# Layer 1 of a four-layer kernel in another order: the first sigmoid ahead of the last latent copy, the recurrence output turned into other banks, gelu two tiles ahead of the rounding

## The chip, the cores and the metric

The kernel runs on one core of a Trainium2 chip. The metric is the device time of one execution in microseconds (us). Each engine (TensorE, here PE; VectorE, DVE; ScalarE, ACT; GpSimd, POOL; and the DMA issuer SP) runs its own instructions in order and waits on semaphores for the others.

## What is computed

Four layers work on `x`, 1024 tokens (4 batches of 256) of 256 channels. Each begins with a recurrence over the tokens (the same `k = v = fside` in all layers, another decay and bonus in each), whose result does not depend on `x`:

```python
base = sigmoid(x) * num / max(den, 1e-8)     # num, den: forward and backward scans plus a bonus term
cond = base * (0.8 + 0.2 * tf)               # tf = sigmoid(sum(time_emb)), one number per batch
x = x + ffn_l(cond)
```

The ffn of layer 0 routes 32 small experts and adds shared ones, that of layer 2 routes 8 experts, that of layer 3 is a ternary gated one. The ffn of layer 1, which the change is about, is

```python
q, s1 = quantize_rowwise(cond)               # round(cond * 127 / absmax of the row)
h = gelu((q @ W1q.T) * (s1 * sW1 / 127**2) + b1)     # 256 -> 1024
q2, s2 = quantize_rowwise(h)                 # the row's absmax over 1024 numbers
y = (q2 @ W2q.T) * (s2 * sW2 / 127**2) + b2          # 1024 -> 256
```

## The kernel before, in words

Everything is written out by hand: the order of each engine's instructions is the order of the code in its block (`sync`, `gpsimd`, `scalar`, `vector`, `tensor`), and semaphores with counts tie the engines together. There are eight PSUM banks of 128x512 f32.

Layer 0 ends in 64 expert units. Unit u uses `bank[u % 4]` for its up-projection; `expert_y` (L1597) adds all units into banks 4 (first half of the tokens) and 5 (second half). `latent_copy(s)` (ACT, L689) copies bank 4+s, `latent_out(s)` (PE, L1612) multiplies it into two banks of two token tiles each, and `add_routed(v)` (DVE, L1121) adds bank v to `x` and counts `x1_ready`, to 4.

Then layer 1 starts. `sigmoid_x(1, (s,))` (ACT, L605) takes the sigmoid of half s of `x`. `turn_gain(1, b)` (PE, L1477) turns batch b's recurrence output back to tokens x channels, in `gain_bank(1, b)`, and `make_cond(1, b)` (DVE, L939) multiplies the two to `cond` (it counts `cond_ready`). `row_scales(s)` (DVE, L1164 to L1167) finds the row maxima of a half, four tiles.

A tile t of 128 tokens (NT = 8 of them) goes through:
- POOL `quant_rows` (L462) rounds it to `qf`; PE `turn_rows` (L1663) turns it into bank 4; ACT `l1_first` (L715) copies it to `qT`; PE `first` (L1676) multiplies it into banks 0, 1 (even t) or 2, 3 (odd t).
- DVE `l1_pre` (L1174, two halves) scales it and adds the bias; ACT `l1_gelu` (L721) writes `gl`.
- DVE `l1_scales` (L1183 to L1186) finds the row maximum; ACT `l1_quant` (L726) rounds `gl` in place; PE `turn_hidden` (L1687) turns it into banks 5 and 6; ACT `l1_second` (L734, two halves) copies it to `q2T`; PE `second` (L1696) multiplies it into bank 7; DVE `l1_out` (L1191) adds it to `x` and counts `x2_ready`.

POOL adds the bias b2 to `x` meanwhile (L473). `xp`, `qf`, `qT`, `q2T` and `gl` have two buffers each. ACT must load a table (ACT_TABLE_LOAD) when it goes from one of exp, sigmoid and gelu to another; copies need none. DVE also finishes here the last block of the recurrence of layers 1 and 2 (`gain_reciprocal` L923 and `gain_out` L929). Behind the last tiles come sigmoid and cond of layer 2 (`sigmoid_pair` L622, `make_cond(2, b)`), whose gains are turned into banks 0 to 3, and its routing, whose first vector instruction is the copy of the logits (L1236). Those go on in one chain to the 23 expert blocks of layer 2.

Of the kernel before, what the change touches and what calls it, by code (L numbers as in the profile page):

```python
# [58 lines left out]
def build(nc, x_d, kt_d, te_d, w_d, u_d, sm_d, gbias_d, down_d, fc2_d, w1_d, w2_d,  # L59
          q1_d, q1b_d, q2_d, q2b_d, rt_d, gu_d, dn_d, t1_d, t2_d, t3_d, cond_d, y_d, cw_d, out_d):  # L60
    with ExitStack() as ctx:
# [802 lines left out]
        def _(dve):  # L864
# [334 lines left out]
            for t in range(-3, NT + 1):  # L1199
                if 0 <= t + 1 < NT and t != 0:  # L1200
                    l1_pre(t + 1)
                if t == -2:
                    add_routed(2)
                    add_routed(3)
                if t == -1:
                    make_cond(1, 2)
                    make_cond(1, 3)
                if 0 <= t < NT:
                    l1_scales(t)
                if t == 0:  # L1210
                    l1_pre(1)
                    row_scales(1)
# [691 lines left out]
```

## Time and profile before

| | |
|---|---|
| time, median of 3 runs | 499.85 us (499.19 to 500.91) |
| the profiled execution | 499.61 us, of it 497.9 us in the profile's span |
| PE busy | 396.2 us, 80% of the span |
| DVE busy | 353.4 us, 71% |
| ACT busy | 229.9 us, 46% |
| POOL busy | 229.9 us, 46% |
| granted TensorE clock, mean of the span | 0.938 of full speed |

Busy time says how long an engine ran instructions, and no engine is busy all the time, so the shares alone do not say what sets the end: in each stage it is a chain that goes from engine to engine. The layer-0 experts run to about 207 us of the span, layer 1 from there to about 260 us, the routing of layer 2 to about 288 us, its expert blocks to about 440 us, and layer 3 to the end.

### The profile page before, as it was taken

The page shows a single profiled execution, that of the slowest core. Times are in us where ns is not written, and L with a number is a line of the kernel's source. Part 1 is how long each engine was busy: PE and PEld are TensorE (multiplying, and loading weights), DVE is VectorE, ACT ScalarE, POOL GpSimd, SP SyncE. Part 2 cuts the span into 40 slices and gives each one's busy share as a digit, 9 for nine tenths or more (in the row PEclk, how much of TensorE's full clock was granted, in tenths as well). Part 3 has the DMA queues.
Part 4 walks back from the last instruction along what each step waited for, and adds up shares of the span by engine and source line. Part 5 has one row for each costly group of instructions (what it writes and reads, how often), then busy time and mean ns, then how long its engine had stood idle before and what let it go on. Part 6 is the DMA issues. An engine that isn't in the chain of part 4 may idle for free.

```text
span 497.9 us, 5689 instructions
## 1 busy us (share of the span) xinstructions
PE 396.2 (80%) x1636; PEld 252.3 (51%) x1636; DVE 353.4 (71%) x643; ACT 229.9 (46%) x448; POOL 229.9 (46%) x313
## 2 busy tenths in 40 slices
PE   0866877999989999856765289999999999914795
PEld 0645655855555555534454135655555555612453
DVE  5999679899999999469854727655655421148995
ACT  4400174266766766537783113333333333235884
POOL 3116140468778996222200145785785551104642
PEclk9998899999999999979995569999999999975999
DMA  7900000536656643000011389889889887150001
GB/s 229 366 1 0 1 0 2 201 127 199 197 195 198 224 149 128 0 1 1 1 44 42 130 301 349 296 297 379 292 284 396 294 279 304 40 180 1 11 33 43
DMA packets 23262, 77.37 MB, mean 155 GB/s; under 512 B 3424, under 2 KB 7904, under 8 KB 19648
## 3 DMA queue, kind: packets, MB, share of 16 engines
q1 hardware_dynamic: 19936, 69.94, 39.4%
q0 software_dynamic: 2208, 6.03, 4.0%
q10 hardware_dynamic: 1088, 1.05, 0.6%
q8 instruction: 13, 0.21, 0.2%
q14 instruction: 17, 0.14, 0.1%
HBM read 71.76 MB, written 5.24 MB: 155 GB/s over the span
## 4 chain that ended last, share of the span: by engine, by line
PE 47%; DVE 33%; issue 7%; ACT 6%; DMA 4%; POOL 1%; SPq 0%; DVEq 0%; ACTq 0%; POOLq 0%
PE bank L1792 17%; PE bank L1812 9%; PE bank L1603 6%; DVE fw L915 4%; DVE hx L1130 4%; DVE bw L918 3%; DVE fw L923 2%; DVE fw L977 2%; PE bank L1803 2%; DVE gl L1418 2%; PE bank L1460 2%; PE bank L1462 2%; PE bank L1461 2%; DVE pt L1425 1%; DVE cond L939 1%
## 5 line engine op out<-in xcount | busy, mean ns | idle before, releaser
L1792 PE MATMUL bank<-gu,xbT 128*128 128x512 f32 x184 | 85.8, 610 | 0.9 <-ACT xbT L774 0.9
L1603 PE MATMUL bank<-hx,w2raw 128*128 128x512 f32 x128 | 67.1, 607 | 4.2 <-DVE hx L1130 3.8
L1333 DVE TENSOR_TENSOR hm<-bank,sl 128x512 f32<-128x512 f32 x23 | 15.9, 691 | 70.7 <-PE bank L1792 39.5
L680 ACT ACTIVATE rl<-bank 128x512 f32<-128x512 f32 x64 | 38.1, 595 | 39.5 <-PE bank L1462 38.8
L1792 PEld LDWEIGHTS bank<-gu,xbT 128*128 128x128 f32 x184 | 35.6, 196 | 37.2 <-issue 34.7
L1460 PE MATMUL bank<-xlhi,w1hi 128*128 128x512 f32 x64 | 49.5, 773 | 1.1 <-DVE hx L958 1.1
L1812 PE MATMUL bank<-dn,hT 128*128 128x256 f32 x184 | 45.2, 388 | 3.5 <-ACT hT L785 0.8
L1130 DVE TENSOR_TENSOR hx<-bank,cwb 128x512 f32<-128x512 f32 x64 | 41.9, 657 | 6.5 <-ACT bank L684 4.8
L490 POOL DMA_INDIRECT y_rows<-yb,dest_i x23 | 25.0, 1088 | 41.6 <-ACT yb L791 41.0
L923 DVE RECIPROCAL fw<-fw 128x256 f32<-128x256 f32 x24 | 41.5, 1730 | 0.0
L415 POOL TENSOR_TENSOR fw<-fw,bw 128x256 f32<-128x256 f32 x32 | 24.1, 752 | 34.7 <-DVE bw L918 34.3
L483 POOL DMA_INDIRECT xb<-cond_rows,row_i x23 | 26.4, 1148 | 28.7 <-PE bank L1778 15.1
L1812 PEld LDWEIGHTS bank<-dn,hT 128*128 128x128 f32 x184 | 33.1, 189 | 11.8 <-issue 8.2
L684 ACT ACTIVATE bank<-rl 128x512 f32<-128x512 f32 x64 | 38.1, 596 | 0.0
L1541 PE MATMUL bank<-fw,ident 128*128 128x256 f32 x32 | 12.9, 493 | 25.4 <-DVE bw L918 12.4
L1603 PEld LDWEIGHTS bank<-hx,w2raw 128*128 128x128 f32 x128 | 22.3, 188 | 16.0 <-DVE hx L1130 10.0
L779 ACT ACTIVATE sl<-bank 128x512 f32<-128x512 f32 x23 | 13.7, 597 | 34.6 <-PE bank L1792 34.6
L785 ACT ACTIVATE hT<-bank 128x256 f32<-128x256 f32 x46 | 15.1, 381 | 29.4 <-PE bank L1803 29.4
L791 ACT ACTIVATE yb<-bank 128x256 f32<-128x256 f32 x23 | 8.8, 384 | 37.2 <-PE bank L1812 37.2
L419 POOL TENSOR_TENSOR fw<-fw,eu 128x256 f32<-128x256 f32 x32 | 23.9, 748 | 3.5
L1687 PE MATMUL bank<-ident,gl 128*128 128x128 f32 x128 | 17.2, 277 | 10.4 <-ACT gl L726 8.3
L1461 PE MATMUL bank<-xllo,w1hi 128*128 128x512 f32 x64 | 25.3, 395 | 0.0
(283 smaller groups left out, 907.7 us busy)
## 6 DMA issues: line engine op xcount, KB each, us to landing
gu<-in_gu SPq DMA_DIRECT2D x23, 1024.0 KB, 7.3
cwb<-cw_rows SPq DMA_DIRECT2D x32, 512.0 KB, 3.8
dn<-in_dn SPq DMA_DIRECT2D x23, 512.0 KB, 4.5
traw<-in_t SPq DMA_DIRECT2D x3, 1024.0 KB, 7.9
w1raw<-in_w SPq DMA_DIRECT2D x8, 256.0 KB, 4.8
w2raw<-in_w SPq DMA_DIRECT2D x8, 256.0 KB, 5.0
kT<-in_kt SPq DMA_DIRECT2D x4, 256.0 KB, 5.5
x<-in_x SPq DMA_DIRECT2D x2, 512.0 KB, 6.9
```

Source lines behind the costliest of these rows:

```text
L415: pool.tensor_tensor(fw[:, p, d, :], fw[:, p, d, :], bw[:, p, d, :], ALU.add).then_inc(sem("both_" + part), 1)
L483: pool.indirect_dma_start(xb[:, b % RING, :], None, cond_d, bass.IndirectOffsetOnAxis(ap=row_i[:, b:b + 1], axis=0)).then_inc(sem(f"xb_in{ ...
L490: pool.indirect_dma_start(y_d, bass.IndirectOffsetOnAxis(ap=dest_i[:, b:b + 1], axis=0), yb[:, b % 2, :], None).then_inc(sem(f"y_out{b % 2 ...
L680: act.activation(rl[:, u % 3, :], bank[u % 4][:], ACT.Relu).then_inc(sem("r_ready"), 1)
L684: act.activation(bank[u % 4][:], rl[:, u % 3, :], ACT.Square).then_inc(sem("sq_ready"), 1)
L923: dve.reciprocal(fw[:, p, 1, :], fw[:, p, 1, :]).then_inc(sem("rden_ready"), 1)
L1130: dve.tensor_tensor(hx[:, 0, u % 4, :], bank[u % 4][:], cwb[:, e % CRING, HALF * s:HALF * s + HALF], ALU.mult).then_inc(sem("h0_ready"), 1)
L1460: pe.matmul(out, lhs[0], rhs[0], start=start, stop=False)
L1461: pe.matmul(out, lhs[0], rhs[1], start=False, stop=False)
L1603: pe.matmul(bank[4 + s][:], w2raw[:, e // 4 % 2, e % 4, :], hx[:, 0, u % 4, :], start=(e == 0), stop=(e == E0 - 1), skip_group_check=True) ...
L1792: ins = pe.matmul(bank[2 * (b % 2) + up][:], xbT[:, b % 2, k, :], gu[:, b % RING, k, up * I2:up * I2 + I2], start=(k == 0), stop=(k == KC ...
L1812: ins = pe.matmul(y_bank(b), hT2[:, b % 2, j, :], dn[:, b % RING, j, :], start=(j == 0), stop=(j == 3))
```

## The change

ACT. The sigmoid table is loaded right behind the last expert's square, and the first half's sigmoid is taken before the second latent copy instead of after it. In the tile loop gelu of tile t+2 comes right behind the rounding of tile t, ahead of the copies of tile t (before: gelu of t+2 behind the copies of t, right ahead of the rounding of t+1). `gl` now has three buffers in layer 1 and `pt` a third column. The table for layer 2's sigmoid is loaded inside the loop, at t = 5, and the sigmoids of its first two batches are taken before the rounding of the last tile.

PE. The gains of layer 1 go to banks 0, 1, 6, 2 (before 2, 3, 5, 6); all four are turned before `latent_out(1)`, two of them between the last `expert_y`. Rows are turned and multiplied one tile further ahead, four tiles instead of three. DVE. `add_routed(2)` and `(3)`, the last reciprocal and `gain_out` stand before the first `l1_pre`, `row_scales(1)` before the first `l1_scales`, and in the loop `l1_scales` and `l1_pre` run one tile further ahead of `l1_out`. POOL waits for the last `expert_y` before it rounds rows.

```diff
-            return bank[((0, 1, 1, 7), (2, 3, 5, 6), (0, 1, 2, 3), (0, 1, 5, 6))[l][b]]
+            return bank[((0, 1, 1, 7), (0, 1, 6, 2), (0, 1, 2, 3), (0, 1, 5, 6))[l][b]]
...
+            pool.wait_ge(sem("y_done"), UNITS)
...
+            load_table(5, ACT.Sigmoid)
+            sigmoid_x(1, (0,))
             latent_copy(1)
-            sigmoid_x(1, (0,))
...
-                wait(act, sem("q2t_ready"), 2 * t - 2)
+                wait(act, sem("q2t_ready"), 2 * t - 4)
                 act.wait_ge(sem("pre_ready"), t + 1)
...
-            for t in range(-2, NT):
+            l1_first(0)
+            sigmoid_x(1, (1,))
+            load_table(1, ACT.Gelu_apprx_tanh)
+            l1_first(1)
+            l1_gelu(0)
+            l1_first(2)
+            l1_gelu(1)
+            l1_first(3)
+            for t in range(NT):
+                l1_quant(t)
                 if t + 2 < NT:
-                    l1_first(t + 2)
-                if t == -2:
-                    sigmoid_x(1, (1,))
-                    load_table(1, ACT.Gelu_apprx_tanh)
-                if t == 0:
-                    l1_quant(t)
-                if 0 <= t + 1 < NT:
-                    l1_gelu(t + 1)
-                if t > 0:
-                    l1_quant(t)
-                if t == NT - 1:
+                    l1_gelu(t + 2)
+                if t + 3 == NT:
+                    load_table(6, ACT.Sigmoid)
+                l1_second(t)
+                if t + 4 < NT:
+                    l1_first(t + 4)
+                if t == NT - 2:
                     sigmoid_pair(2, 0)
                     sigmoid_pair(2, 1)
-                if t >= 0:
-                    l1_second(t)
...
-                wait(dve, sem("q2_ready"), t - 1)
+                wait(dve, sem("q2_ready"), t - 2)
+                wait(dve, sem("x2_ready"), t - 2)
                 dve.wait_ge(sem("gelu_ready"), t + 1)
...
+            add_routed(2)
+            add_routed(3)
+            gain_reciprocal(3 * NBLK - 1, 1)
+            gain_out(3 * NBLK - 1, 2, NBLK - 1, 1)
+            l1_pre(0)
+            make_cond(1, 2)
+            make_cond(1, 3)
+            l1_pre(1)
+            row_scales(1)
+            l1_scales(0)
+            l1_pre(2)
+            for t in range(NT):
+                if t + 1 < NT:
+                    l1_scales(t + 1)
+                if t + 3 < NT:
+                    l1_pre(t + 3)
                 if t >= 1:
                     l1_out(t - 1)
...
-                if u == UNITS - 2:
-                    turn_gain(1, 0)
-            turn_gain(1, 1)
+                if u >= UNITS - 3 and u < UNITS - 1:
+                    turn_gain(1, u - UNITS + 3)
+            turn_gain(1, 2)
+            turn_gain(1, 3)
             latent_out(1)
-            pe.wait_ge(sem("x1_ready"), 3)
-            turn_gain(1, 2)
-            pe.wait_ge(sem("x1_ready"), 3)
-            turn_gain(1, 3)
...
+            pe.wait_ge(sem("x1_ready"), 1)
             turn_rows(0, "", "q1_ready")
+            l1_up(0)
+            turn_rows(1, "", "q1_ready")
+            pe.wait_ge(sem("cond_ready"), 8)
+            l1_up(1)
+            turn_rows(2, "", "q1_ready")
+            l1_up(2)
+            turn_rows(3, "", "q1_ready")
+            l1_up(3)
+            pe.wait_ge(sem("x1_ready"), 4)
+            for t in range(NT):
+                turn_hidden(t, "", "q2_ready")
+                if t + 4 < NT:
+                    turn_rows(t + 4, "", "q1_ready")
                 if t == NT - 2:
                     pe.wait_ge(sem("pre_ready"), NT)
-                    turn_gain(2, 0)
...
+                second(t, "", "x2_ready", lambda c: q2w[:, c, :])
+                if t + 4 < NT:
+                    l1_up(t + 4)
```

What stands in a row on ACT where layer 1 starts, before, from the square of the last expert unit on (`ylat` is the latent copy, `cond<-x` the sigmoid of a half, `qT` the copy of turned rows, `gl<-xp` gelu, `gl<-gl,pt` the rounding):

```order
L684 ACTIVATE bank3<-rl_100 128x512 [waits r_ready]
L689 ACTIVATE ylat_107<-bank5 128x512 [waits y_done]
L605 ACT_TABLE_LOAD
L605 ACTIVATE cond_57<-x_50 128x1024 [waits x1_ready]
L715 ACTIVATE qT_121<-bank4 128x256 [waits q1t_ready]
L605 ACTIVATE cond_57<-x_50 128x1024 [waits x1_ready]
L588 ACT_TABLE_LOAD
L588 ACTIVATE table_65<-wl_67 128x1
L715 ACTIVATE qT_121<-bank4 128x256 [waits q1t_ready]
L721 ACTIVATE gl_123<-xp_122 128x1024 [waits pre_ready]
L715 ACTIVATE qT_121<-bank4 128x256 [waits m1_ready,q1t_ready]
L726 ACTIVATE gl_123<-gl_123,pt_77 128x1024 [waits q2_scale]
```

And in the changed kernel, from the same square on (every line number is up to 5 higher here):

```order
L685 ACTIVATE bank3<-rl_100 128x512 [waits r_ready]
L589 ACT_TABLE_LOAD
L589 ACTIVATE table_65<-wl_67 128x1
L606 ACTIVATE cond_57<-x_50 128x1024 [waits x1_ready]
L690 ACTIVATE ylat_107<-bank5 128x512 [waits y_done]
L717 ACTIVATE qT_121<-bank4 128x256 [waits q1t_ready]
L606 ACTIVATE cond_57<-x_50 128x1024 [waits x1_ready]
L589 ACT_TABLE_LOAD
L589 ACTIVATE table_65<-wl_67 128x1
L717 ACTIVATE qT_121<-bank4 128x256 [waits q1t_ready]
L723 ACTIVATE gl_123<-xp_122 128x1024 [waits pre_ready]
L717 ACTIVATE qT_121<-bank4 128x256 [waits m1_ready,q1t_ready]
```

The table load and the first sigmoid have moved ahead of the second latent copy, and the sigmoid no longer stands behind a wait for the last `expert_y`. The next place is ACT in the tile loop, from one rounding to the next, before:

```order
L726 ACTIVATE gl_123<-gl_123,pt_77 128x1024 [waits q2_scale]
L734 ACTIVATE q2T_124<-bank5 128x512 [waits q2t_ready,m2_ready]
L734 ACTIVATE q2T_124<-bank6 128x512 [waits q2t_ready]
L715 ACTIVATE qT_121<-bank4 128x256 [waits m1_ready,q1t_ready]
L721 ACTIVATE gl_123<-xp_122 128x1024 [waits pre_ready,q2t_ready]
L726 ACTIVATE gl_123<-gl_123,pt_77 128x1024 [waits q2_scale]
```

And in the changed kernel:

```order
L728 ACTIVATE gl_123<-gl_123,pt_77 128x1024 [waits q2_scale]
L723 ACTIVATE gl_123<-xp_122 128x1024 [waits pre_ready,q2t_ready]
L736 ACTIVATE q2T_124<-bank5 128x512 [waits q2t_ready,m2_ready]
L736 ACTIVATE q2T_124<-bank6 128x512 [waits q2t_ready]
L717 ACTIVATE qT_121<-bank4 128x256 [waits m1_ready,q1t_ready]
L728 ACTIVATE gl_123<-gl_123,pt_77 128x1024 [waits q2_scale]
```

Gelu has moved from ahead of the rounding to behind it: it now lies between the rounding of a tile and the copies of that tile, for which PE has to turn the tile. The third place is DVE where layer 1 starts, before, from the adds of the second half (`x<-bank5`) to the first row maximum of gelu's output and the pre-activation behind it:

```order
L1121 TENSOR_TENSOR x_50<-bank5,x_50 128x512 [waits fo_ready,dve_step]
L1121 TENSOR_TENSOR x_50<-bank7,x_50 128x512 [waits fo_ready]
L1174 SCALAR_TENSOR_TENSOR xp_122<-bank0,st_76,b1bc_63 128x512 [waits m1_ready]
L1174 SCALAR_TENSOR_TENSOR xp_122<-bank1,st_76,b1bc_63 128x512
L939 SCALAR_TENSOR_TENSOR cond_57<-bank5,tfb_71,cond_57 128x512 [waits sig_ready,G_turned]
L939 SCALAR_TENSOR_TENSOR cond_57<-bank6,tfb_71,cond_57 128x512 [waits sig_ready,G_turned]
L1183 TENSOR_REDUCE pt_77<-gl_123 128x1 [waits gelu_ready]
L1184 RECIPROCAL pt_77<-pt_77 128x1 [waits dve_step]
L1185 TENSOR_SCALAR pt_77<-pt_77,ws_78 128x1 [waits dve_step]
L1186 TENSOR_SCALAR pt_77<-pt_77 128x1
L1174 SCALAR_TENSOR_TENSOR xp_122<-bank2,st_76,b1bc_63 128x512 [waits m1_ready]
L1174 SCALAR_TENSOR_TENSOR xp_122<-bank3,st_76,b1bc_63 128x512
```

And in the changed kernel:

```order
L1126 TENSOR_TENSOR x_50<-bank5,x_50 128x512 [waits fo_ready,dve_step]
L1126 TENSOR_TENSOR x_50<-bank7,x_50 128x512 [waits fo_ready]
L928 RECIPROCAL fw_55<-fw_55 128x256 [waits sum_den]
L934 SCALAR_TENSOR_TENSOR GT_53<-fw_55 128x256 [waits rden_ready,sum_num]
L1179 SCALAR_TENSOR_TENSOR xp_122<-bank0,st_76,b1bc_63 128x512 [waits m1_ready]
L1179 SCALAR_TENSOR_TENSOR xp_122<-bank1,st_76,b1bc_63 128x512
L944 SCALAR_TENSOR_TENSOR cond_57<-bank6,tfb_71,cond_57 128x512 [waits sig_ready,G_turned]
L944 SCALAR_TENSOR_TENSOR cond_57<-bank2,tfb_71,cond_57 128x512 [waits sig_ready,G_turned]
L1179 SCALAR_TENSOR_TENSOR xp_122<-bank2,st_76,b1bc_63 128x512 [waits m1_ready]
L1179 SCALAR_TENSOR_TENSOR xp_122<-bank3,st_76,b1bc_63 128x512
L1169 TENSOR_REDUCE st_76<-cond_57 128x4 [waits cond_ready]
L1170 RECIPROCAL st_76<-st_76 128x4 [waits dve_step]
```

Behind these rows come two small ones of `row_scales(1)` and then the first `l1_scales`. So the reciprocal, its output step, the pre-activation of tile 1 and the row scales of the second half have all moved ahead of it.

## Rows read from the trace of the kernel before

**Rows 1.** Busy times in windows of the span; after PE's come the clock and DMA.
```profile
212.00:214.00 2.00, 0.00 (x0) 0.00 (x0) 1.90 (x5) 0.00 (x0) 0.29 (x1) 0.61 0.00 0
...
218.00:219.00 1.00, 1.00 (x4) 0.38 (x2) 0.00 (x0) 0.98 (x2) 0.00 (x0) 0.50 0.00 0
...
240.00:250.00 10.00, 7.72 (x56) 5.28 (x56) 8.37 (x16) 7.77 (x13) 0.00 (x0) 1.00 0.00 0
```

**Rows 2.** Timeline of the start of layer 1: start us, us, instruction, idle and releaser.
```profile
202.32 1.11 ACT L684 ACTIVATE bank<-rl 128x512 f32<-128x512 f32 x2
...
204.15 1.28 DVE L1121 TENSOR_TENSOR x<-bank,x 128x512 f32<-128x512 f32 x2
...
206.37 1.02 PE L1603 MATMUL bank<-hx,w2raw 128*128 128x512 f32 x2
...
207.43 0.60 ACT L689 ACTIVATE ylat<-bank 128x512 f32<-128x512 f32 x1 [3.99 <-PE bank L1603]
...
208.04 1.28 ACT L605 ACT_TABLE_LOAD   x1
...
208.08 1.99 PE L1612 MATMUL bank<-fc2w,ylat 128*128 128x256 f32 x8 [0.25 <-ACT ylat L689]
...
209.34 1.06 ACT L605 ACTIVATE cond<-x 128x1024 f32<-128x1024 f32 x1
...
210.53 1.41 DVE L939 SCALAR_TENSOR_TENSOR cond<-bank,tfb,cond 128x512 f32<-128x512 f32 x2 [5.11 <-ACT cond L605]
...
211.98 1.22 DVE L1164 TENSOR_REDUCE st<-cond 128x4 f32<-128x1024 f32 x1
...
213.78 1.29 DVE L1121 TENSOR_TENSOR x<-bank,x 128x512 f32<-128x512 f32 x2
```

**Rows 3.** Timeline of the first two tiles of layer 1.
```profile
217.40 1.89 PE L1676 MATMUL bank<-q1w,qT 128*128 128x512 bf16 x4 [0.48 <-ACT qT L715]
...
219.32 1.41 DVE L1174 SCALAR_TENSOR_TENSOR xp<-bank,st,b1bc 128x512 f32<-128x512 f32 x2 [4.25 <-PE bank L1676]
...
220.13 1.04 PE L1676 MATMUL bank<-q1w,qT 128*128 128x512 bf16 x4 [0.57 <-ACT qT L715]
...
221.97 1.21 DVE L1183 TENSOR_REDUCE pt<-gl 128x1 f32<-128x1024 f32 x1
...
223.72 1.15 ACT L726 ACTIVATE gl<-gl,pt 128x1024 f32<-128x1024 f32 x1 [1.62 <-DVE pt L1186]
...
229.78 1.15 ACT L726 ACTIVATE gl<-gl,pt 128x1024 f32<-128x1024 f32 x1 [0.52 <-DVE pt L1186]
```

**Rows 4.** Timeline of the last reciprocal of the recurrence, on DVE.
```profile
233.01 1.74 DVE L923 RECIPROCAL fw<-fw 128x256 f32<-128x256 f32 x1
...
235.20 0.48 DVE L1191 SCALAR_TENSOR_TENSOR x<-bank,pt,x 128x256 f32<-128x256 f32 x1
```

**Rows 5.** Timeline of a tile in the middle of the loop, from rounding to rounding.
```profile
242.80 1.16 ACT L726 ACTIVATE gl<-gl,pt 128x1024 f32<-128x1024 f32 x1
...
244.76 1.09 ACT L734 ACTIVATE q2T<-bank 128x512 bf16<-128x512 f32 x2 [0.80 <-PE bank L1687]
...
245.50 1.03 PE L1696 MATMUL bank<-q2w,q2T 128*128 128x256 bf16 x8 [0.18 <-ACT q2T L734]
...
245.73 0.39 ACT L715 ACTIVATE qT<-bank 128x256 bf16<-128x256 f32 x1
...
246.00 1.07 ACT L721 ACTIVATE gl<-xp 128x1024 f32<-128x1024 f32 x1
...
246.94 1.16 ACT L726 ACTIVATE gl<-gl,pt 128x1024 f32<-128x1024 f32 x1
```

**Rows 6.** Timeline of the end of layer 1 and the first copy of layer 2's logits.
```profile
255.10 1.28 ACT L622 ACT_TABLE_LOAD   x1
...
259.25 0.48 DVE L1191 SCALAR_TENSOR_TENSOR x<-bank,pt,x 128x256 f32<-128x256 f32 x1 [0.71 <-PE bank L1696]
...
269.61 0.22 DVE L1236 COPY lgs<-bank 128x64 f32<-128x64 f32 x1 [6.27 <-PE bank L1735]
```

More of the change, by code:

```diff
@@ L107, in build @@
         b2bc = sb("b2bc", [P, C])
-        table = sb("table", [P, 5])
+        table = sb("table", [P, 7])
         te = sb("te", [P, B, 64])
@@ L718, in l1_gelu @@
                 p = t % 2
-                wait(act, sem("q2t_ready"), 2 * t - 2)
+                wait(act, sem("q2t_ready"), 2 * t - 4)
                 act.wait_ge(sem("pre_ready"), t + 1)
-                act.activation(gl[:, p, :], xp[:, p, :], ACT.Gelu_apprx_tanh).then_inc(sem("gelu_ready"), 1)
+                act.activation(gl[:, t % 3, :], xp[:, p, :], ACT.Gelu_apprx_tanh).then_inc(sem("gelu_ready"), 1)
             def l1_quant(t):
-                p = t % 2
+                p = t % 3
                 act.wait_ge(sem("q2_scale"), t + 1)
@@ L1190, in l1_out @@
                 dve.wait_ge(sem("xb_ready"), t + 1)
-                dve.scalar_tensor_tensor(out=x[:, t, :], in0=bank[7][:, 0:C], scalar=pt[:, 3, t % 2:t % 2 + 1],
+                dve.scalar_tensor_tensor(out=x[:, t, :], in0=bank[7][:, 0:C], scalar=pt[:, 3, t % 3:t % 3 + 1],
                                          in1=x[:, t, :], op0=ALU.mult, op1=ALU.add).then_inc(sem("x2_ready"), 1)
@@ L1198, in _ @@
             row_scales(0)
[L1199 to L1212, printed above, removed]
-                if t == 2:
-                    gain_reciprocal(3 * NBLK - 1, 1)
-                    gain_out(3 * NBLK - 1, 2, NBLK - 1, 1)
+            add_routed(2)
[14 more added lines that the diff above has]
+                    l1_pre(t + 3)
                 if t >= 1:
                     l1_out(t - 1)
-                if t == NT - 1:
-                    make_cond(2, 0)
-                    make_cond(2, 1)
+            make_cond(2, 0)
+            make_cond(2, 1)
+            l1_out(NT - 1)
             make_cond(2, 2)
@@ L1472, in turn_gain @@
                     pe.wait_ge(sem("y_ready"), NB)
-                elif b >= 2 and l < 2:
-                    pe.wait_ge(sem("cond_ready"), 4 * l + b - 1)
+                elif l == 0 and b == 3:
+                    pe.wait_ge(sem("cond_ready"), 2)
+                elif l == 1 and b == 2:
+                    pe.wait_ge(sem("x1_ready"), 2)
                 for u in range(2):
@@ L1686, in turn_hidden @@
                         c = 4 * h + j
-                        ins = pe.transpose(bank[5 + h][:, j * P:j * P + P],
-                                           gl[:, t % (3 if tag else 2), c * P:c * P + P], ident[:])
+                        ins = pe.transpose(bank[5 + h][:, j * P:j * P + P], gl[:, t % 3, c * P:c * P + P], ident[:])
                     ins.then_inc(sem("q2t_ready" + tag), 1)
@@ L1699, in _, with l1_up @@
             w_first = [lambda k, h=h: q1w[:, k, 512 * h:512 * h + 512] for h in range(2)]
+            def l1_up(t):
+                first(t, "", w_first, lambda p: (2 * p, 2 * p + 1))
+            pe.wait_ge(sem("x1_ready"), 1)
             turn_rows(0, "", "q1_ready")
[L1701 to L1706 removed]
+            l1_up(0)
[11 more added lines that the diff above has]
+                    turn_rows(t + 4, "", "q1_ready")
                 if t == NT - 2:
                     pe.wait_ge(sem("pre_ready"), NT)
[L1710 to L1719 removed]
+                    for b in range(B):
+                        turn_gain(2, b)
+                second(t, "", "x2_ready", lambda c: q2w[:, c, :])
+                if t + 4 < NT:
+                    l1_up(t + 4)
             def turn_cond2(b):
```

19 lines of the change are left out of this document (2 added, 17 removed).

## Prediction
> **What bounds the kernel now.** I read the windows of the span first, then the timeline of layer 1 from the last expert to the logits of layer 2, following from each instruction that had waited to what released it. The window in the tile loop shows PE busy 7.72, DVE 8.37 and ACT 7.77 us of 10 at full clock [rows 1]: no engine is full, so a chain between engines sets the pace. Three pieces of it are what the change touches.
>
> The start [rows 2]: the last `expert_y` ends at 207.39, the latent copy follows, then a sigmoid table and the first sigmoid, to 210.40. DVE has waited 5.11 us for it. Yet the half of `x` that this sigmoid reads was complete at 205.43 (204.15 + 1.28), and ACT had been free since 203.43. So this stretch is order, not work. From there conds, row scales and the first tile lead to the first rounding at 223.72 [rows 3], my first mark.
>
> The first tiles [rows 3]: from the rounding of tile 0 to that of tile 1 there are 6.06 us, since between the two `l1_scales` DVE does two pre-activations and the second half's row scales.
>
> The loop [rows 5]: a tile takes 4.14 us, 242.80 to 246.94, and on ACT it is closed: rounding 1.16, then idle 0.80 while PE turns the tile, copies 0.97 (244.76 to 245.73), the row copy 0.27, gelu 0.94. At the end a table load (255.10) lies between the last tile's rounding and its copies; the last `l1_out` starts at 259.25, and the first logits copy follows 10.36 later [rows 6].
>
> **The change part by part.** I take marks and lay the changed order out with the durations of the rows. Instructions of one engine that don't wait overlap by some 0.1 us, as gelu's 0.94 between starts shows; a handover costs 0.04, on PE's multiplications 0.14.
>
> *Start to the first rounding.* ACT: table 1.28 and the small activation 0.2 from 203.43, free at 204.93, so the sigmoid starts when `x` is there, 205.47, ends 206.55. PE turns two gains between the experts (0.43 each, so the last `expert_y` ends at 207.83 instead of 207.39; that is the price of moving them, and it delays only the second half). DVE: conds 206.59 to 208.0, row scales 1.80 (211.98 to 213.78 before) to 209.8. Rows reach PE at 210.3, where `latent_out(1)`, 207.83 + copy 0.64 + 1.99, is just done at 210.5. This is 4 us earlier than before. Then DVE becomes late: adds to 211.2, reciprocal and its output 2.19 [rows 4], so `l1_pre(0)` only at 213.4 although its product is there at 212.5; 1.33 for it, 1.40 for conds 2 and 3, to 216.1. Now the new banks cost something: the product of tile 1 writes bank 2, which holds the gain of batch 3, and has to wait for that cond: 216.1 + 0.14 + 1.04 = 217.3 (a PE that has stood idle since about 212.7). Then `l1_pre(1)` 1.33, row scales 1.80, `l1_scales(0)` 1.71 (221.97 to 223.68 before) give 222.2 for the first rounding. **Gain 1.5 us**, of the 4 that the sigmoid won; the rest is work brought ahead, paid back next.
>
> *Rounding 0 to rounding 1.* Ahead of `l1_scales(1)` now lies only `l1_pre(2)`. Scales end at 225.1, and ACT has rounding 0, gelu 2 (from 223.5, after `l1_pre(2)`), copies and row copy to do first: 223.5 + 0.95 + 0.97 + 0.27 = 225.7. That is 3.5 us instead of 6.06: **gain 2.5**.
>
> *Rounding 1 to rounding 5*, before 229.78 to 246.94, 17.16 us, the reciprocal of rows 4 in it. With gelu in ACT's gap, ACT alone would need 1.03 + 0.95 + 0.97 + 0.27 = 3.2, and DVE 1.33 + 1.63 + 0.40 = 3.4 per tile. But another loop closes. `second(t)` writes bank 7 and waits for `l1_out(t-1)`, and in the new order `l1_out` stands behind `l1_pre(t+3)`, whose product comes on PE behind `second(t-1)`. Its length: `second` 1.03 less 0.15 of overlap, product 1.04, `l1_pre` 1.33, `l1_out` 0.48, handovers 0.16: **3.9 us a tile**. Laid out, the roundings come at 225.7, 229.0 (ACT's own 3.3), 233.7 (4.7, for `l1_out(0)` stands behind two scales and two pre-activations and ends at 229.8), 237.6, 241.2: 15.5 us. **Gain 1.7**.
>
> *Rounding 5 to the last `l1_out`*, before 12.31. The third table load, 1.28 + 0.1, moves from behind the last rounding to ahead of the copies of tile 5, with nothing to cover it there; the two sigmoids (1.06) lie ahead of the last rounding instead of behind it. Rounding 6 at 245.6, rounding 7 at 249.6, last `l1_out` at 253.4: 12.2. **Gain 0.1**: the stretch loses in front what it wins behind. Conds 0 and 1 of layer 2 are then made ahead of the last `l1_out`, as before. The rest, 10.36 to the logits copy, keeps its order, and I cost it at nothing. POOL's new wait costs nothing, since its rounding waits for row scales later than that anyway; the third `gl` buffer costs no time.
>
> Sum 1.5 + 2.5 + 1.7 + 0.1 = 5.8, with the roundings 5.9.
>
> **The clock.** Before, PE did nothing in 212 to 214, granted clock 0.61, and the first tile's product ran at 0.50 in 1.89 us; the next took 1.04 [rows 1, 3]. In the changed kernel PE stands idle 3.6 us from 212.7. If the clock then drops to the lower level (1.2 of 2.4 GHz), the product of tile 1 costs 0.85 more on the path: gain 5.0. If it does not, 5.9. The Trainium skill ("TensorE: Matmul & The Clock Gate", Part 1) says that the throttled clock is the default and activity releases it, which speaks for a drop here; row and rule agree that an idle PE comes first. I take the middle, 5.4.
>
> **Table loads, weighed.** The row of the load shows 1.28 between copy end 208.03 and sigmoid start 209.34: nothing further [rows 2]. The Trainium skill ("ScalarE: Activation LUTs", "What ACT_TABLE_LOAD costs") adds a drain of about 1.38 us to its 1.28 for every switch. By the row the sum stays; by the page about 1.4 would be added at the load inside the loop and 0.7 at the start, a gain near 3.4.
>
> The profiled execution took 499.61, 0.24 under the median of 499.85. 499.61 - 5.4 = 494.2; against the median 494.45. I say 494.3.
>
> **The rivals.**
> A, as laid out: 493.5 to 495.2. Chance 0.62.
> B, the loop does not get shorter: some wait that I can't see keeps 4.14 a tile, the lag of `l1_out` for instance. Then the gain is 1.5 + (6.06 - 4.14) + (17.16 - 4 x 4.14) + 0.1 = 4.1 at full clock, 3.2 with the drop: 495.6 to 496.4. For it: banks 0 to 3 and 7 are still single. Against: the gap of 0.80 on ACT is filled. Chance 0.14.
> C, a load stalls ACT by more than its row, say its 1.28 once more in the loop and 0.7 at the start, since it now follows gelu with no pause and a copy waits right behind: gain 3.4, 496.1. Against: the row of the load before, with 0.01 on either side. The page named above is the one that would have it so. Chance 0.04.
> D, the loop runs at DVE's own 3.4 a tile because handovers on the bank-7 loop are shorter: 2 us more gain, or later stages fall better to the clock: 492.3 to 493.5. Chance 0.12.
> E, slower: the clock falls in the loop. The bank-7 loop holds 1.9 us of PE work, which doubles: 3.9 becomes 5.8 a tile. Three tiles at that level eat the gain (3 x 1.9 = 5.7), the five from tile 2 on would give 499.6 - 5.4 + 9.5 = 503.7. Against: in the loop before the clock is 1.00 with PE busy 77% [rows 1], and its share rises with 3.9 instead of 4.14. Chance 0.03.
> F, no change: the expert blocks of layer 2 start late for another reason, or fall worse to the clock by as much. Chance 0.05; speaks against it that from `l1_out` to the logits copy is one chain [rows 6].
>
> **How the numbers follow.** Time of A, 494.3. The range leaves out E, F and the far end of D, and takes in the two ends of the clock, B and C: 492.7 to 496.5. What a measurement here can tell from no change is about 0.3%, 1.5 us; A to D all lie beyond. Faster 0.92, same 0.05, slower 0.03.
>
> **What would show it.** First sigmoid at about 205.5; conds at 206.6; DVE without its 5.11 wait; PE idle some 3.5 us before the product of tile 1, released by cond; first rounding at 222.2 to 223.1; no wait of ACT for the turned tile or little; `second` waiting for `l1_out`; roundings 3.9 apart in the middle; a table load ahead of the copies of tile 5; last `l1_out` at 253.4 to 254.3. It is wrong if the roundings stay 4.1 apart, if `l1_pre(0)` doesn't find DVE late, or if the clock is at 0.50 beyond the first tile.

## The result and the profile after

The changed kernel takes 495.31 us in the median of 11 runs (492.86 to 497.70), the kernel before 500.36 in the runs beside it (498.89 to 502.61). The ratio is 0.9905, with a 95% interval of 0.9881 to 0.9929: 0.95% or 4.75 us faster, more than the 0.3% that can be told from no change. The forecast was 494.3 (492.7 to 496.5). The profiled execution took 494.82 us, its span 493.1, where that of before had 499.61. Two timed runs that lie over 1.5% above the fastest of their kernel, at a lower mean clock, are left out of every ratio and median below: one of the kernel before (507.44 us) and one of e2 (566.60 us).

The first section of its page (busy time, share of the span, instructions):

```profile
PE 397.6 (81%) x1630; PEld 255.4 (52%) x1636; DVE 355.6 (72%) x643; ACT 230.4 (47%) x450; POOL 230.8 (47%) x313
```

Busy times are as before to within some 2 us: work was moved, not removed. Its timeline at the start of layer 1:

```profile
203.21 1.11 ACT L685 ACTIVATE bank<-rl 128x512 f32<-128x512 f32 x2
204.34 1.28 ACT L589 ACT_TABLE_LOAD   x1
205.04 1.28 DVE L1126 TENSOR_TENSOR x<-bank,x 128x512 f32<-128x512 f32 x2
205.63 0.20 ACT L589 ACTIVATE table<-wl 128x1 f32<-128x1 f32 x1
206.35 1.06 ACT L606 ACTIVATE cond<-x 128x1024 f32<-128x1024 f32 x1 [0.52 <-DVE x L1126]
207.55 1.41 DVE L944 SCALAR_TENSOR_TENSOR cond<-bank,tfb,cond 128x512 f32<-128x512 f32 x2 [1.23 <-ACT cond L606]
208.75 0.60 ACT L690 ACTIVATE ylat<-bank 128x512 f32<-128x512 f32 x1 [1.34 <-PE bank L1610]
...
212.04 1.74 DVE L928 RECIPROCAL fw<-fw 128x256 f32<-128x256 f32 x1
...
217.21 1.33 PE L1678 MATMUL bank<-q1w,qT 128*128 128x512 bf16 x4 [3.64 <-DVE cond L944]
...
219.44 1.89 PE L1678 MATMUL bank<-q1w,qT 128*128 128x512 bf16 x4 [0.48 <-ACT qT L717]
...
223.46 1.15 ACT L728 ACTIVATE gl<-gl,pt 128x1024 f32<-128x1024 f32 x1 [1.47 <-DVE pt L1192]
```

The sigmoid now waits for `x` and for nothing else; DVE's wait for it has shrunk from 5.11 us [rows 2] to 1.23. The reciprocal of [rows 4] stands at 212.04, ahead of the first tile, and PE is idle for 3.64 us until a cond frees the bank of tile 1's product. A tile in the middle of the loop, in the same timeline:

```profile
234.95 1.16 ACT L728 ACTIVATE gl<-gl,pt 128x1024 f32<-128x1024 f32 x1
235.08 1.05 PE L1697 MATMUL bank<-q2w,q2T 128*128 128x256 bf16 x8 [0.81 <-DVE x L1197]
235.97 1.03 PE L1678 MATMUL bank<-q1w,qT 128*128 128x512 bf16 x4
235.99 1.06 ACT L723 ACTIVATE gl<-xp 128x1024 f32<-128x1024 f32 x1
237.03 1.41 DVE L1179 SCALAR_TENSOR_TENSOR xp<-bank,st,b1bc 128x512 f32<-128x512 f32 x2 [0.19 <-PE bank L1678]
237.53 1.08 ACT L736 ACTIVATE q2T<-bank 128x512 bf16<-128x512 f32 x2 [0.47 <-PE bank L1689]
238.35 0.48 DVE L1197 SCALAR_TENSOR_TENSOR x<-bank,pt,x 128x256 f32<-128x256 f32 x1
238.76 1.16 ACT L728 ACTIVATE gl<-gl,pt 128x1024 f32<-128x1024 f32 x1
238.89 1.05 PE L1697 MATMUL bank<-q2w,q2T 128*128 128x256 bf16 x8 [0.80 <-DVE x L1197]
```

3.81 us from rounding to rounding (234.95, 238.76), where [rows 5] had 4.14. `second` (L1697) waits 0.8 us for `l1_out` (L1197), and a ring, a chain of waits that ends where it began, closes in those rows: 0.89 to the product, 1.06 to `l1_pre`, 1.32 to `l1_out`, 0.54 to the next `second`. And the end of the loop:

```profile
244.42 1.28 ACT L589 ACT_TABLE_LOAD   x1
245.82 1.06 ACT L736 ACTIVATE q2T<-bank 128x512 bf16<-128x512 f32 x2
246.55 1.03 PE L1697 MATMUL bank<-q2w,q2T 128*128 128x256 bf16 x8 [1.93 <-ACT q2T L736]
...
248.91 1.91 PE L1484 MATMUL bank<-ident,GT 128*128 128x128 f32 x16
...
254.51 0.48 DVE L1197 SCALAR_TENSOR_TENSOR x<-bank,pt,x 128x256 f32<-128x256 f32 x1 [0.98 <-PE bank L1697]
...
264.88 0.23 DVE L1241 COPY lgs<-bank 128x64 f32<-128x64 f32 x1 [6.27 <-PE bank L1741]
```

The windows of the same stretches (columns as in [rows 1]) show the clock at 0.72 and 0.58 around the first tiles and at 1.00 in the loop:

```profile
216.00:222.00 6.00, 3.88 (x12) 1.63 (x12) 4.47 (x9) 2.75 (x4) 0.37 (x1) 0.72 0.00 1
224.00:228.00 4.00, 3.25 (x16) 2.91 (x17) 3.93 (x9) 3.54 (x6) 0.71 (x2) 0.58 0.01 2
240.00:250.00 10.00, 6.65 (x54) 5.38 (x53) 6.57 (x17) 8.69 (x13) 0.00 (x0) 1.00 0.00 1
```

All profiles are compared below by the same marks. "First" is the time from the end of the last expert's square on ACT (203.43 before, 204.32 after) to the rounding of tile 0; the next columns run from rounding 0 to 1, from 1 to 5, from there to the start of the last `l1_out`, and from that to the first logits copy. The last column is the timed ratio to the kernel before, with its interval. It comes from several runs of each kernel, the marks from one execution each, so the two need not agree.

| kernel | first | 0 to 1 | 1 to 5 | 5 to last out | to logits | ratio |
|---|---|---|---|---|---|---|
| before | 20.29 | 6.06 | 17.16 | 12.31 | 10.36 | 1 |
| after | 19.14 | 4.02 | 14.82 | 12.21 | 10.37 | 0.9905 (0.9881 to 0.9929) |
| e8_changed_again | 19.69 | 3.74 | 15.17 | 12.20 | 10.37 | 0.9919 (0.9893 to 0.9944) |
| e1_start_only | 13.46 | 6.07 | 17.16 | 12.30 | 10.25 | 0.9877 (0.9835 to 0.9919) |
| e7_sigmoid_behind | 24.06 | 3.50 | 15.16 | 13.17 | 9.62 | 0.9971 (0.9946 to 0.9995) |
| e9_light_front | 14.48 | 6.11 | 15.09 | 12.21 | 10.37 | 0.9865 (0.9842 to 0.9887) |
| e3_gelu_behind | 18.95 | 4.73 | 16.37 | 14.32 | 10.69 | 0.9967 (0.9941 to 0.9992) |
| e2_out_first | 19.70 | 4.02 | 13.40 | 13.10 | 9.70 | 0.9862 (0.9814 to 0.9910) |
| e5_table_at_end | 19.70 | 4.02 | 15.28 | 11.46 | 9.83 | 0.9866 (0.9839 to 0.9893) |
| e4_busy_pe | 18.86 | 4.02 | 14.79 | 13.41 | 11.30 | 0.9881 (0.9835 to 0.9928) |
| e10_ring_closed | 13.48 | 7.30 | 14.47 | 11.73 | 10.48 | 0.9843 (0.9820 to 0.9867) |
| e6_all_three | 13.46 | 6.62 | 12.91 | 12.38 | 9.33 | 0.9808 (0.9772 to 0.9843) |

After against before the marks give 1.15 + 2.04 + 2.34 + 0.10 = 5.63 us up to the last `l1_out`, and nothing behind it. The square ended 0.89 later in this execution (clock 0.89 in the first 60 us of the span against 0.94 before, in a stretch that the change doesn't touch), which leaves the 4.8 us between the two spans to within 0.1.

### The profile page after: what moved, and what is told of

It is laid out like the page before. It is cut to its first block, busy times and chain, and to the rows that moved or that the text cites. A ratio compares the mean times of both kernels' runs of the same rounds, so it can differ in the third digit from the quotient of the medians.

```text
span 493.1 us, 5685 instructions
## 1 busy us (share of the span) xinstructions
PE 397.6 (81%) x1630; PEld 255.4 (52%) x1636; DVE 355.6 (72%) x643; ACT 230.4 (47%) x450; POOL 230.8 (47%) x313
## 3 DMA queue, kind: packets, MB, share of 16 engines
q10 hardware_dynamic: 1088, 1.05, 0.6%
## 4 chain that ended last, share of the span: by engine, by line
PE 34%; DVE 9%; ACT 4%; issue 2%; DMA 2%; POOL 1%; DVEq 0%; ACTq 0%; POOLq 0%
PE bank L1798 17%; PE bank L1818 9%; PE bank L1809 2%; DVE gl L1423 2%; DVE pt L1430 1%; PE bank L1697 1%; PE bank L1741 1%; PE bank L1784 1%; ACT q2T L736 1%; DVE x L1377 1%; PE bank L1689 1%; DMA xb<-cond_rows,row_i 1%; DMA gy<-y_rows 1%; ACT gl L728 1%; PE bank L1678 1%
## 5 line engine op out<-in xcount | busy, mean ns | idle before, releaser
L1467 PE MATMUL bank<-xlhi,w1lo 128*128 128x512 f32 x64 | 25.2, 394 | 0.0
```

The source lines that it names most:

```text
L1467: return pe.matmul(out, lhs[1], rhs[0], start=False, stop=stop)
```

## The experiments

e1 to e4 ran beside one another, so did e5 to e8, and so did e9 and e10, each set with runs of the kernel before. The changed kernel is in the second set only (e8); against the others it is compared through the kernel before.

**The new start alone.** The kernel before with the new place of the sigmoid, the new banks and turns, and POOL's wait, but with all its own loops and its own DVE order.

```diff
+            pool.wait_ge(sem("y_done"), UNITS)
...
+            load_table(5, ACT.Sigmoid)
             sigmoid_x(1, (0,))
+            latent_copy(1)
...
             turn_gain(1, 2)
             turn_gain(1, 3)
+            latent_out(1)
```

> The kernel before with the new start alone: sigmoid ahead of the latent copy, the gains in banks 0, 1, 6, 2 and turned between the experts; every loop in its old order. Theory (the start wins some 5 us at the first row scales, and the new order of the vector engine spends it again by bringing other work ahead of the first rounding): the first rounding comes 6 to 7 us earlier than before and the loop keeps its 4.14 us a tile, so 6 to 7 us less than before, 1 to 2 us below the changed kernel. Rival (the parts of the change add up, the loop order is worth its 2.5 + 1.7 us as in my sum): the start alone gives 1.5 us, some 498.5.

493.50 us, ratio 0.9877 (0.9835 to 0.9919): in time not told apart from the whole change, whose interval overlaps it. By the marks it is 1.3 us shorter than the whole change (59.24 against 60.56 us from the square to the logits copy). Its timeline:

```profile
206.70 1.06 ACT L606 ACTIVATE cond<-x 128x1024 f32<-128x1024 f32 x1 [0.52 <-DVE x L1123]
...
211.78 0.41 PE L1662 MATMUL bank<-ident,qf 128*128 128x128 f32 x2
...
213.74 1.41 DVE L1176 SCALAR_TENSOR_TENSOR xp<-bank,st,b1bc 128x512 f32<-128x512 f32 x2 [1.26 <-PE bank L1675]
...
216.38 1.21 DVE L1185 TENSOR_REDUCE pt<-gl 128x1 f32<-128x1024 f32 x1
216.52 1.04 PE L1675 MATMUL bank<-q1w,qT 128*128 128x512 bf16 x4 [2.60 <-DVE cond L941]
218.13 1.15 ACT L728 ACTIVATE gl<-gl,pt 128x1024 f32<-128x1024 f32 x1
```

DVE goes from the conds straight to the row maximum of tile 0 (216.38), and the first rounding comes 6.83 us earlier than before; the loop behind it is the old one to the hundredth in its sum (17.16). So the new start is worth 6.8 us at this mark, where the whole change shows 1.15.

The sigmoid is only the largest part of these 6.8 us, as distances from the end of the square show. The first cond starts at 3.23 instead of 7.10, which is 3.9 us for the sigmoid. The rows of tile 0 are turned at 7.11 instead of 12.86, a further 1.9 us: in the kernel before POOL had begun to round them at 213.71, but PE first turned the gains of batches 2 and 3, which waited for an add on DVE and which the new banks let it turn earlier.

```profile
213.71 0.94 POOL L462 TENSOR_SCALAR qf<-cond,st 128x256 f32<-128x256 f32 x2 [11.24 <-DVE st L1166]
...
214.53 1.97 PE L1477 MATMUL bank<-ident,GT 128*128 128x128 f32 x8 [4.46 <-DVE x L1121]
...
216.29 0.63 PE L1663 MATMUL bank<-ident,qf 128*128 128x128 f32 x2
```

The last 1.1 us lie between those turned rows and the first pre-activation (1.96 instead of 3.03), where the granted clock was 1.00 in 212 to 216 in this run and 0.51 in the same piece before (216.29 to 219.32). No run moves the turns of the gains alone, so this split is read from two traces and not tested.

**The new loops without the early sigmoid.**

```diff
-            load_table(5, ACT.Sigmoid)
-            sigmoid_x(1, (0,))
             latent_copy(1)
+            sigmoid_x(1, (0,))
```

> The changed kernel with the first sigmoid and its table load behind the latent copy again, all else new. Theory (the early sigmoid is on the chain with its full length and the new loop order brings about nothing beside it): first rounding 4 us later, total 3.5 to 4.5 us above the changed kernel, within 1.5 us of the kernel before. Rival (the sigmoid is worth 1.5 us as the first term of my sum could be read, the loops 4.3): 1.5 us above the changed kernel.

497.96 us, ratio 0.9971, against 0.9919 of the changed kernel in the same set, with intervals just apart (from 0.9946 here, to 0.9944 there). The difference of the medians is 2.0 us, less than expected; one trace of each differs by 4.3 us at the marks. The first rounding comes at 24.06, 3.8 us later than before, although the first pre-activation starts 1.4 us earlier (14.48 behind the square instead of 15.89). So what now stands on DVE ahead of that rounding costs 5.2 us in this execution, with the product of tile 1 at the lower clock level (1.89 us) in it. The quicker loops win that back and little more: without the early sigmoid 0.3% of the change's 0.8% in this set is left.

**A light front.** The changed kernel with the first `l1_scales` ahead of the second tile's pre-activation and of `row_scales(1)`, the first rounding ahead of the second gelu, and the reciprocal with its output back in the loop, at t = 5.

```diff
+            l1_quant(0)
             l1_gelu(1)
...
-            gain_reciprocal(3 * NBLK - 1, 1)
-            gain_out(3 * NBLK - 1, 2, NBLK - 1, 1)
...
+            l1_scales(0)
             l1_pre(1)
...
-            l1_scales(0)
...
+                if t == 5:
+                    gain_reciprocal(3 * NBLK - 1, 1)
+                    gain_out(3 * NBLK - 1, 2, NBLK - 1, 1)
```

> The changed kernel with the light front alone: first l1_scales right behind the conds of the second half, pre-activation of tile 1 and row scales behind it, the reciprocal at t = 5 of the loop, rounding 0 on ACT ahead of gelu 1. Theory (the work brought ahead of the first rounding costs its length there and is hidden further back): first rounding 5.5 us earlier than in the changed kernel, 3 us of that taken back at once at the next tile, 2 us left at the end; some 493.5. Rival (what is brought ahead must be done anyway and VectorE sets the pace): within 0.5 us of the changed kernel.

492.38 us, ratio 0.9865, its interval (0.9842 to 0.9887) clear of that of the changed kernel's second set of runs (0.9893 to 0.9944) and just overlapping that of its first (from 0.9881), both in other sets. First rounding at 14.48 instead of 19.14 and 19.69; of these 5 us, 2.1 to 2.4 are given back at once (0 to 1 takes 6.11 again), the rest stays: the last `l1_out` is 2.3 us earlier than after. The first mark is 1.0 us behind e1's because of the product of tile 1 at the lower clock level, 1.89 where e1 has 1.04. The row copy that stands on ACT ahead of the rounding waits for the turn behind that product, which is slower too (0.63 instead of 0.38):

```profile
215.71 1.89 PE L1681 MATMUL bank<-q1w,qT 128*128 128x512 bf16 x4 [2.60 <-DVE cond L946]
```

**Gelu behind the copies again.** ACT's loop in the order rounding, copies, row copy, gelu; the rest as changed.

```diff
                 l1_quant(t)
+                l1_second(t)
+                if t + 4 < NT:
+                    l1_first(t + 4)
                 if t + 2 < NT:
                     l1_gelu(t + 2)
```

> The changed kernel with gelu of tile t+2 behind the copies of tile t, as before. Theory (ACT's gap of 0.8 us while PE turns the tile was the cost of the old loop): a tile takes 4.1 us again with a wait of 0.8 us ahead of the copies, the time is 2 to 2.7 us above the changed kernel. Rival (bank 7 alone sets the pace, whatever ACT does): under 1 us.

498.61 us, ratio 0.9967, 0.5 to 0.6% above the changed kernel (0.9919, 0.9905); its interval from 0.9941 on is clear of the first set of the changed kernel's and overlaps the second by a little. The tiles are 4.18 us apart, and DVE's row maximum now waits for gelu:

```profile
235.08 1.16 ACT L728 ACTIVATE gl<-gl,pt 128x1024 f32<-128x1024 f32 x1
235.33 1.22 DVE L1189 TENSOR_REDUCE pt<-gl 128x1 f32<-128x1024 f32 x1 [0.75 <-ACT gl L723]
...
237.09 1.08 ACT L736 ACTIVATE q2T<-bank 128x512 bf16<-128x512 f32 x2 [0.85 <-PE bank L1689]
...
239.27 1.16 ACT L728 ACTIVATE gl<-gl,pt 128x1024 f32<-128x1024 f32 x1
```

ACT's idle gap of 0.85 ahead of the copies is back. So gelu in the gap is what shortens the tile, by 0.37 us, and it is needed: the other parts of the new loop alone keep the old pace. Not all of the loss is the pace of the tiles: of 4.5 us at the marks against the changed kernel's first trace, 2.1 lie behind rounding 5, where the table load now delays rounding 6 (5.40 us instead of 4.48) and the turns of layer 2's gains ran at a lower clock (3.35 instead of 1.91).

**`l1_out` ahead of `l1_pre` on DVE**, which takes `l1_pre` out of the ring through bank 7.

```diff
-                if t + 3 < NT:
-                    l1_pre(t + 3)
                 if t >= 1:
                     l1_out(t - 1)
+                if t + 3 < NT:
+                    l1_pre(t + 3)
```

> The changed kernel with l1_out ahead of l1_pre in the loop of the vector engine. Theory (the loop is bound by bank 7: second, product, l1_pre, l1_out in a ring, 3.8 us a tile): with l1_out first the ring is open, a tile takes 3.3 to 3.4 us, 2 us less than the changed kernel in all. Rival (ACT or DVE are already full at 3.8 us a tile): no change, within 0.5 us.

494.38 us in the median of five runs (491.50 to 496.21), ratio 0.9862 with a wide interval; against the changed kernel inconclusive. The trace is not:

```profile
235.18 1.19 ACT L728 ACTIVATE gl<-gl,pt 128x1024 f32<-128x1024 f32 x1
...
237.94 1.03 PE L1697 MATMUL bank<-q2w,q2T 128*128 128x256 bf16 x8 [0.21 <-ACT q2T L736]
...
238.41 1.19 ACT L728 ACTIVATE gl<-gl,pt 128x1024 f32<-128x1024 f32 x1
```

`second` no longer waits for `l1_out` but for ACT's copy, and three tiles in a row take 3.20, 3.23 and 2.96 us instead of 3.8 and 3.5. The ring was the bound of the loop. In this execution the gain was lost again, 0.6 in a later first rounding and 0.9 behind rounding 5, both times with PE at the lower clock: the product of tile 1 took 1.89 instead of 1.33, the turn of tile 6 1.97 instead of 1.10. Behind the last `l1_out` 0.7 came back, for the clock too, as the rows under "Light front, table at the end, ring open" show.

**The table load out of the loop**, back behind the last rounding, with the two sigmoids.

```diff
-                if t + 3 == NT:
-                    load_table(6, ACT.Sigmoid)
+                if t == NT - 1:
+                    sigmoid_pair(2, 0)
+                    sigmoid_pair(2, 1)
...
-                if t == NT - 2:
-                    sigmoid_pair(2, 0)
-                    sigmoid_pair(2, 1)
```

> The changed kernel with the third table load and the two sigmoids between the last rounding and its copies, as before. Theory (the load inside the loop costs its 1.3 us with nothing over it, lets TensorE stand 1.9 us, after which its clock has fallen in two traces, and wins at the end only the wait of the last copies): roundings 5 to 7 come 1.3 to 2.4 us earlier, the last l1_out 1 us earlier, total 1 us below the changed kernel, more where the clock had fallen. Rival (the place of the load is neutral, as my sum had it with 0.1): within 0.5 us.

493.05 us, ratio 0.9866 against 0.9919 of the changed kernel in the same set; the intervals just touch (0.9893). PE's wait for the copies of tile 5 is 0.68 instead of 1.93, and roundings 5 to 7 are 3.22 and 2.93 apart instead of 4.48 and 3.96:

```profile
244.63 1.03 PE L1695 MATMUL bank<-q2w,q2T 128*128 128x256 bf16 x8 [0.68 <-ACT q2T L736]
```

The last stretch ends 0.75 earlier, less than those two intervals win, because the load then lies behind the last rounding (248.96), as it did before. Against the repeat the marks show 0.9 us in all, 0.5 of it the clock behind the last `l1_out`, where the medians differ by 2.9. So the place of the load is worth some 0.75 us by the traces; that it is worth the whole 0.5% is not shown.

**The changed kernel once more**, to see how far its own traces scatter.

> The changed kernel itself, as the base for the others of this call. From its first trace: 5.6 us less than before from the last expert's square to the logits copy. If that stretch is all that changed, its time is 4.5 to 6 us under the kernel before here too; single executions scatter by some 2 us because the clock falls at other places in them.

495.95 us, ratio 0.9919. The tiles from rounding 2 to 5 agree with the first trace to 0.01, the marks ahead of them do not: 19.69 against 19.14 at the first rounding, which is the product of tile 1 at 1.89 instead of 1.33. And the last expert's square, up to which both executions run the same instructions, ended at 207.10 instead of 204.32.

**A busy PE.** 32 turns of the identity into bank 3, which nobody reads, stand ahead of the wait for the conds.

```diff
+            for _ in range(32):
+                pe.transpose(bank[3][:, 0:P], ident[:], ident[:])
             pe.wait_ge(sem("cond_ready"), 8)
```

> The changed kernel with 32 turns of the identity into the free bank 3 while TensorE waits for the cond of batch 3, work that nobody uses. Theory (the idle 3.6 us let the clock fall to 0.50, which costs 0.85 us at the product of tile 1 and some more in the first tiles): the clock stays at 1.00 through layer 1 and the time falls by 1 to 1.5 us. Rival (the lower clock is hidden behind DVE): no change, within 0.5 us.

493.83 us, ratio 0.9881: inconclusive, the runs lie at 492.6 to 493.9 and at 498.6 to 498.8, and the one profiled is the slowest of them. The clock is 1.00 in 216 to 222 and the products of tiles 1 and 2 take 1.04 each. Then it falls at the next idle stretch instead, and once more behind the table load, where the turns of layer 2's gains (L1484) take 3.21 us, not 1.91:

```profile
215.98 1.04 PE L1678 MATMUL bank<-q1w,qT 128*128 128x512 bf16 x4
...
223.23 1.94 PE L1689 MATMUL bank<-ident,gl 128*128 128x128 f32 x8 [2.31 <-ACT gl L728]
...
245.00 1.03 PE L1697 MATMUL bank<-q2w,q2T 128*128 128x256 bf16 x8 [1.93 <-ACT q2T L736]
...
247.73 3.21 PE L1484 MATMUL bank<-ident,GT 128*128 128x128 f32 x16
```

The fill saves 0.28 us at the first rounding (0.83 against the repeat), less than the 1 to 1.5 expected; in this execution the fall is put off, not avoided.

**Light front, table at the end, ring open**, the edits of e9, e5 and e2 together, and the same with the ring closed again (`l1_out` behind `l1_pre`).

> New start, light front on the vector engine (first l1_scales right behind the conds; pre-activation of tile 1, row scales and reciprocal behind it, the reciprocal at t = 5), l1_out ahead of l1_pre, gelu in the gap, table load at the end. Theory (all four costs found are real and separate): first rounding 6.8 us earlier than before, tiles of 3.3 to 3.4 us from tile 2 on, last l1_out some 4.5 us before that of the changed kernel, total 489.5 to 491.5. Rival (the vector engine is now full and the gains overlap): 492 to 493.5, no better than the start alone.

> The kernel of the run with all three (light front, gelu in the gap, table at the end), but l1_out behind l1_pre again. Theory (the ring through bank 7 is the pace): tiles of 3.8 to 3.9 us from tile 2 on instead of 3.3, 2 to 3 us above the run with all three. Rival (ACT or VectorE is the pace there anyway): within 0.5 us of it.

489.52 us with the ring open, ratio 0.9808: 1.9% faster than before, and 1.1% faster than the changed kernel in the same set, with intervals that lie apart. 491.07 with it closed, ratio 0.9843. In the middle of the loop the open ring runs at 3.34 a tile, the closed one at 3.80:

```profile
228.57 1.05 PE L1698 MATMUL bank<-q2w,q2T 128*128 128x256 bf16 x8 [0.34 <-DVE x L1197]
228.91 1.16 ACT L728 ACTIVATE gl<-gl,pt 128x1024 f32<-128x1024 f32 x1
...
231.91 1.05 PE L1698 MATMUL bank<-q2w,q2T 128*128 128x256 bf16 x8 [0.34 <-DVE x L1197]
232.25 1.16 ACT L728 ACTIVATE gl<-gl,pt 128x1024 f32<-128x1024 f32 x1
```

In the closed one, the same wait in the same view:

```profile
230.24 1.05 PE L1698 MATMUL bank<-q2w,q2T 128*128 128x256 bf16 x8 [0.80 <-DVE x L1197]
```

0.3 us of wait is left with the ring open, since `l1_out` still stands behind `l1_scales`. Of the 1.56 us that the open ring wins from rounding 1 to 5, 0.65 go again behind rounding 5: there the reciprocal at t = 5 makes the last `l1_scales` late on DVE, and roundings 6 and 7 are 3.87 apart instead of 3.19. The two totals differ by 0.35%, less than expected and with intervals that overlap; that the ring costs this much in time is likely, and shown only in the traces.

What e2, e5, e6 and e7 save between the last `l1_out` and the logits copy (0.67, 0.54, 1.04 and 0.75 us) is the clock on PE. The second group of products for the logits took 1.88 us before and after, and 1.22, 1.34, 1.06 and 1.12 in those four; in e6 a turn behind it is 0.2 shorter as well. In the 2.5 us around it the granted clock was 0.50 after (259.0 to 261.5) and 0.85 in e6 (252.0 to 254.5). The row of the changed kernel:

```profile
259.39 1.88 PE L1741 MATMUL bank<-rtraw,cT 128*128 128x8 f32 x8 [0.69 <-ACT cT L763]
```

The same row in e6:

```profile
252.59 1.06 PE L1742 MATMUL bank<-rtraw,cT 128*128 128x8 f32 x8 [0.69 <-ACT cT L763]
```

## Why the prediction was right

It was right in its time, its sign and its mechanism. The sizes of three terms were off, by -0.35, -0.46 and +0.64 us; that they cancel is luck.

*Start, forecast 1.5, measured 1.15 and 0.60 (first trace and repeat).* The layout held: sigmoid at 2.03 behind the square instead of 2.04, DVE late at `l1_pre(0)`, PE idle 3.64 instead of 3.6 and released by cond, and the product of tile 1 at a partly lowered clock (1.33, between 1.04 and 1.89). What the prediction called "work brought ahead, paid back next" was right as a sum and too kind as a judgement. It also undervalued the start: it had the rows reach PE at 210.5, where they come (7.11 behind the square, so 210.54), but called this 4 us earlier than before, the sigmoid's share, and left out that the rows before had stood behind two turns of gains until 216.29. e1 shows 6.8 us for the new start, so the new DVE order spends 5.7 of them ahead of the first rounding. Of them only the 2.0 of the interval 0 to 1 come back for it; the shorter 1 to 5 is there in e9 too, without the heavy front. The change could have had some 2 to 2.7 us more (0.9905 or 0.9919 against 0.9865).

*Rounding 0 to 1, forecast 2.5, measured 2.04; 1 to 5, forecast 1.7, measured 2.34.* Together 4.2 and 4.38. The first interval was 4.02 instead of 3.5, because PE's clock was low around it, 0.58 in 224 to 228 (the turn of tile 0 took 1.94, that of tile 1 then 1.04); I had kept the clock apart as a term at the start. In e7, where the turn of tile 0 took 1.06, the interval is 3.50. From rounding 0 to rounding 3 the forecast was 11.5 and the trace has 11.49; the repeat has 11.55 and e5, with the same order up to there, 11.95, so the hundredth is chance. Then 3.81 and 3.54 for 3.9 and 3.6. The ring through bank 7 was named as the bound, and e2, e6 and e10 show that it is: take `l1_pre` out of it and the tile takes 3.0 to 3.3 us in the traces.

*Rounding 5 to the last `l1_out`, forecast 0.1, measured 0.10*, and 10.36 to the logits copy became 10.37. Up to the experts nothing changed behind it: the first expert product of layer 2 is 19.26 behind the logits copy, 19.36 before.

*The clock.* The middle of two cases, 5.4, stood against a timed 4.75 and 5.6 by the marks. One of the prediction's own signs of being wrong did come: the clock was at 0.50 beyond the product of tile 1 as well (0.50 in 218 to 220, the product of tile 2 in 1.89 us at 219.44). That product cost nothing, since its pre-activation waited for DVE until 223.34; the turn of tile 0 cost the half microsecond of the interval 0 to 1. Which case an execution falls in is no property of the kernel: after the same 3.64 us of idle PE the product of tile 1 took 1.33 in the first trace and 1.89 in the repeat, and e9 has it at 1.89, e10, with the same front, at 1.04.

*The rivals.* B, the loop stays at 4.14: refuted, and e3 shows under which condition it would have come true (4.18, with gelu outside the gap). C, the table load stalls ACT: refuted. The loads stand at 204.34 and 244.42 with 1.28 each, and what follows them starts 0.01 later (205.63, 245.71). The rule of the Trainium skill that the prediction weighed ("ScalarE: Activation LUTs", "What ACT_TABLE_LOAD costs"), a drain of about 1.38 us at each switch, isn't seen in this case's rows. But the load inside the loop isn't free, since nothing covers its 1.28 there: e5, without it, is 0.5% faster in time, of which the marks show 0.75 us. The prediction had that stretch as "loses in front what it wins behind"; measured, it loses 0.75 us more than it has to. E, the clock falls in the loop: in none of the traces; between 234 and 242 the windows show 1.00 in all of them, and it falls at both ends of the loop. D and F were not needed.

Open stays whether another bank for the gain of batch 3, so that the product of tile 1 need not wait for its cond, would remove PE's idle stretch. It wasn't tried. Open too is how the 6.8 us of the new start divide between the sigmoid and the turns of the gains when each is moved alone.

## What to carry to other kernels

Work that is brought ahead of the first item of a pipeline costs its time there, less what its engine had been waiting (2.4 us of reciprocal and output made the first pre-activation 1.05 us later than in e1, where DVE had waited 1.26), and the pipeline pays back only the part that had stood on its own closing path: lay out the first item separately, and try each part of such a change alone before the whole, as one part (e1 here) can bring as much as all of them together. In a loop over engines look for the ring through the one resource with a single buffer, and keep every instruction that need not be in it out of it on the in-order engines; swapping two neighbours on DVE gave 0.5 us a tile in the traces, though no clear difference in time. A table load belongs where its engine is idle anyway.

## What the runs showed of the hardware

The granted clock falls around idle stretches of PE as short as 1.9 to 3.6 us inside a stage that is otherwise at 1.00, in some executions and not in others. Five traces have the same order up to the product of tile 1 and the same 3.64 us of idle PE ahead of it; it took 1.33 (after), 1.89 (e8, e2, e5) and 1.14 us (e3). Behind the 1.9 us wait at the table load the clock was 0.57 to 0.67 in the next 4 us window in the traces of e2, e4 and e7, and the 16 turns took 2.42 to 3.21 us; in those of after, e8 and e9, with the same wait, they took 1.91. In e3 the wait was 2.86 us, the clock 0.62 and the turns took 3.35.

Executions of one kernel lie up to 5 or 6 us apart (492.86 to 497.70 us for the changed one), as much as the change is worth. The last expert's square, up to which the order is the same in all twelve profiles, ended between 202.21 (e10) and 207.10 us (e8), with a clock of 0.97 and 0.89 in the first 60 us. That the clock makes the whole of that scatter is likely and not shown. At half a per cent only many runs decide, or the marks of the trace where the clock around them is the same.
